# Two sets of edges, the second sorted on VectorE between the additions of the first set's chunks

## The chip, the cores and the metric

The kernel runs on one core of a Trainium2 chip. The metric is the device time of one execution, in microseconds (us). The core has four engines that compute: TensorE (PE in the profile), VectorE (DVE), ScalarE (ACT) and GpSimd (POOL); SyncE (SP) only issues DMAs. Each runs its own queue of instructions in order and waits on semaphores for the others.

## The reference

A graph attention layer with a residual and a layer norm: 6250 nodes of 128 features, 206250 edges in no order of use to the kernel.

```python
wn_out = n_out @ W_lin + b_lin
e_ij = leaky_relu2(jnp.concatenate([n_in, n_out], axis=-1) @ W_att + b_att)
a_ij = (e_ij @ w_alpha)[:, 0]
seg_max = jax.ops.segment_max(a_ij, recv, num_segments=N_NODES)
a_exp = jnp.exp(a_ij - seg_max[recv])
denom = jax.ops.segment_sum(a_exp, recv, num_segments=N_NODES)
alpha = a_exp / jnp.maximum(denom[recv], 1e-12)
n_i = jax.ops.segment_sum(alpha[:, None] * wn_out, recv, num_segments=N_NODES)
return jax.nn.elu(n_i)
...
x = _layernorm(x + _L0_gnn_ref(x, edge_attr_128, edge_index_t, L0_gnn_W_lin, L0_gnn_b_lin, L0_gnn_W_att, L0_gnn_b_att, L0_gnn_w_alpha), axis=-1)
```

## The kernel before

The receivers are 49 blocks of 128 nodes. The kernel sorts the edges by the receiver's block, so that each unit of 128 places in the sorted order belongs to one block, and then goes through the units in order, four at a time (a chunk of 512 places).

**Ahead of the loop.** The edges are packed as keys in a tile of 128 partitions by 2048 columns. VectorE sorts it by a bitonic network of min and max operations: phases 1 to 10 inside groups of columns, then 14 runs. An even run compares across all columns (11 stages, most of them in two halves, `within`); an odd run compares across partitions (run s of them has s stages), for which PE turns the tile by transposes and ScalarE copies it back (`piece_out`), half by half. `compare` issues one min and one max; `compare_groups` two of each over half as many elements. Within run 0 stands `make_padding`: ScalarE has counted the edges of each block in 49 passes (`count_pass`), PE has summed the counts, and VectorE works out how many pad places each block needs; the pads go through DRAM into the key tile. At the same time PE and ScalarE make a table in DRAM, for each node its part of the hidden vector and its `wn_out` (`project`, `copy_pqv`), and the receivers' part in SBUF, which is split into three bf16 parts by VectorE and ScalarE during the sort (`split_p`).

**The loop.** 415 chunks; each engine has its own `step(i, j)`, run for chunk k = 8 i + j by `chunks`: eight steps written out, a hardware loop of eight steps a body, and the last seven written out. The engines work on different chunks in the same step:
- GpSimd: `gather`, four indirect DMAs that fetch the table's rows of 512 senders into `rows`, a ring of eight chunks. It waits for `indexed` and for `high_sums_done` of the chunk eight before.
- PE: `high_sums(k)`, `hidden(k + 4)`, `turn_weights(k + 1)`, `mask(k + 3)`, `low_sums(k + 1)`, `spread_lanes(k + 6)`. `hidden` waits for the gathered rows.
- ScalarE: `weigh(k + 2)`, `slope(k + 4)`, `copy_weights(k + 1)`, `lessen(k + 2)` (two activations), `stage_index(k + 9)`.
- VectorE: `lowest(k + 2)`, the first addition `add_sums(k, 0)`, `new_peaks(k + 2)` (a scan), the second addition, `leaky_relu(k + 3)`, the third addition, `grow(k + 2)`, `make_onehot(k + 5)`, the fourth addition. An addition scales and adds one unit's sums (from PSUM) into `sums` of its block.

The last units hold only pads, whose senders all point to one block of 128 rows of the table. Behind the loop come the division, elu, the residual and the layer norm, block by block.

Lines of the profile: L412 is `gather`'s indirect DMA; L1020 lowest, L1028 the scan, L1036 `grow`, L1012 `leaky_relu`, L1006 `make_onehot`, L1049 an addition; L899 and L900 are min and max of `compare`, L907 and L908 of `compare_groups`; L644 turns a piece of the tile, L493, L494 and L487 copy it back; L431 counts, L614 and L615 are `project`; L825 begins `make_padding`; L991 to L996 unpack the sorted keys at the end of the sort.

## Time and profile before

| | us |
|---|---|
| median of 3 runs (2672.36 to 2678.7) | 2672.62 |
| the profiled execution's own time | 2676.63 |
| its span, first to last instruction | 2674.9 |
| PE busy | 2265.2 (85%) |
| VectorE busy | 1938.0 (72%) |
| ScalarE busy | 1338.6 (50%) |
| GpSimd busy | 1584.3 (59%) |

The busy times are of one profiled execution. Issuing and waiting are not counted as busy, and the ends of matmuls are modelled. The clock that TensorE was granted is 2.4 GHz in nearly the whole loop (1.0 in the profile) and 1.2 GHz (0.5) from about 250 to 530 us.

### The profile page before, as it was taken

The page shows a single profiled execution, that of the slowest core. Times are in us where ns is not written, and L with a number is a line of the kernel's source. Part 1 is how long each engine was busy: PE and PEld are TensorE (multiplying, and loading weights), DVE is VectorE, ACT ScalarE, POOL GpSimd, SP SyncE. Part 2 cuts the span into 40 slices and gives each one's busy share as a digit, 9 for nine tenths or more (in the row PEclk, how much of TensorE's full clock was granted, in tenths as well). Part 3 has the DMA queues.
Part 4 walks back from the last instruction along what each step waited for, and adds up shares of the span by engine and source line. Part 5 has one row for each costly group of instructions (what it writes and reads, how often), then busy time and mean ns, then how long its engine had stood idle before and what let it go on. Part 6 is the DMA issues. An engine that isn't in the chain of part 4 may idle for free.

```text
span 2674.9 us, 67073 instructions
## 1 busy us (share of the span) xinstructions
PE 2265.2 (85%) x13543; PEld 1535.4 (57%) x13752; DVE 1938.0 (72%) x4727; ACT 1338.6 (50%) x4146; POOL 1584.3 (59%) x1674
## 2 busy tenths in 40 slices
PE   3991211199999999999999999999999999999981
PEld 1330111166666666666666666666666666666661
DVE  7978999866666666666666666666666666666667
ACT  3772111055555555555555555555555555555545
POOL 0000000277777777777777777777777777777760
PEclk9998555599999999999999999999999999999996
DMA  4110000043333333333333333333333333333361
GB/s 103 39 41 19 0 0 0 22 108 105 105 106 104 105 105 104 106 105 105 106 104 105 105 104 106 105 105 106 105 105 105 104 105 106 104 106 105 105 93 50
DMA packets 96368, 235.57 MB, mean 88 GB/s; under 512 B 27935, under 2 KB 41205, under 8 KB 96135
## 3 DMA queue, kind: packets, MB, share of 16 engines
q0 software_dynamic: 79744, 218.60, 31.3%
q1 hardware_dynamic: 16594, 16.65, 2.2%
q8 instruction: 10, 0.16, 0.0%
q14 instruction: 20, 0.16, 0.0%
HBM read 225.32 MB, written 9.82 MB: 88 GB/s over the span
## 4 chain that ended last, share of the span: by engine, by line
PE 80%; DVE 11%; issue 4%; DMA 2%; POOL 2%; ACT 1%; DVEq 0%; SPq 0%; POOLq 0%; ACTq 0%
PE hidden_ps L675 24%; PE turned_ps L702 14%; PE masked_ps L686 14%; PE turned_ps L693 8%; PE hidden_ps L672 8%; DVE keys_i L900 4%; DVE keys_i L899 4%; PE turned_ps L660 3%; PE hidden_ps L615 3%; PE hidden_ps L614 2%; PE masked_ps L685 2%; POOL rows L412 2%; DMA rows<-qv_table,index 1%; DMA x_sb<-in_x 1%; PE masked_ps L608 1%
## 5 line engine op out<-in xcount | busy, mean ns | idle before, releaser
L412 POOL DMA_INDIRECT rows<-qv_table,index x1660 | 1576.1, 949 | 557.5 <-issue 476.5
L531 ACT ACTIVATE keys_i<-masked_ps,peaks 128x128 f32<-128x128 f32 x1660 | 474.5, 368 | 602.4 <-DVE peaks L1028 602.4
L675 PE MATMUL hidden_ps<-onehotT,p_part 128*128 128x128 bf16 x4980 | 740.4, 220 | 1.4
L1020 DVE TENSOR_REDUCE unit_low<-masked_ps 128x4 f32<-128x512 f32 x415 | 287.1, 692 | 594.8 <-PE masked_ps L686 594.8
L675 PEld LDWEIGHTS hidden_ps<-onehotT,p_part 128*128 x4980 | 472.2, 96 | 275.5 <-issue 205.1
L702 PEld LDWEIGHTS turned_ps<-rows,keys_i 128*128 128x128 f32 x3320 | 456.8, 190 | 299.5 <-issue 269.3
L1049 DVE SCALAR_TENSOR_TENSOR sums<-sums,shrink,turned_ps 128x129 f32 x1660 | 572.5, 345 | 66.3 <-issue 2.9
L702 PE MATMUL turned_ps<-rows,keys_i 128*128 128x129 f32 x3320 | 523.0, 280 | 15.1 <-issue 11.6
L672 PE MATMUL hidden_ps<-identf,rows 128*128 128x128 f32 x1660 | 470.4, 283 | 15.7 <-DMA rows<-qv_table,index 10.7
L686 PE MATMUL masked_ps<-leaky,w_cols 128*128 128x512 f32 x830 | 424.9, 593 | 10.9
L522 ACT ACTIVATE keys_i<-hidden_ps 128x512 f32<-128x512 f32 x415 | 247.9, 597 | 319.7 <-PE hidden_ps L675 319.5
L1006 DVE TENSOR_SCALAR onehotT<-turned_ps,part_f 128x512 bf16<-128x512 f32 x415 | 309.3, 745 | 13.8 <-PE turned_ps L660 7.5
L1012 DVE TENSOR_TENSOR leaky<-hidden_ps,keys_i 128x512 f32<-128x512 f32 x415 | 283.8, 684 | 0.0
L693 PE MATMUL turned_ps<-identf,keys_i 128*128 128x128 f32 x1660 | 261.0, 280 | 0.5
L672 PEld LDWEIGHTS hidden_ps<-identf,rows 128*128 128x128 f32 x1660 | 231.6, 140 | 44.2 <-issue 28.7
L550 ACT ACTIVATE keys_i<-turned_ps 128x512 f32<-128x512 f32 x415 | 247.9, 597 | 5.7 <-PE turned_ps L693 3.6
L644 PE MATMUL turned_ps<-identf,keys_i 128*128 128x128 f32 x208 | 50.0, 420 | 234.0 <-DVE keys_i L900 197.0
L693 PEld LDWEIGHTS turned_ps<-identf,keys_i 128*128 128x128 f32 x1660 | 174.6, 141 | 20.8 <-issue 2.3
L644 PEld LDWEIGHTS turned_ps<-identf,keys_i 128*128 128x128 f32 x208 | 39.9, 220 | 243.8 <-DVE keys_i L900 170.2
L686 PEld LDWEIGHTS masked_ps<-leaky,w_cols 128*128 128x128 f32 x830 | 158.2, 191 | 15.6
L660 PE MATMUL turned_ps<-lane_rows,identb 128*128 128x512 bf16 x414 | 157.5, 380 | 5.1 <-DVE onehotT L1006 5.1
L398 POOL MEMSET sums<- 128x6321 f32 x1 | 5.4, 5367 | 235.1 <-ACT p_part L507 235.1
(133 smaller groups left out, 1618.5 us busy)
## 6 DMA issues: line engine op xcount, KB each, us to landing
rows<-qv_table,index POOLq DMA_INDIRECT x1660
qv_table<-qv_out SPq DMA_DIRECT2D x49, 128.5 KB, 2.3
out<-x_sb SPq DMA_DIRECT2D x1, 1344.0 KB
recv_mem<-unit_blocks SPq DMA_DIRECT2D x1, 896.0 KB, 5.2
out<-x_sb SPq DMA_DIRECT2D x1, 896.0 KB
keys_i<-in_src SPq DMA_DIRECT2D x1, 768.0 KB
keys_i<-in_dst SPq DMA_DIRECT2D x1, 768.0 KB
recv_mem<-in_src SPq DMA_DIRECT2D x1, 604.5 KB
```

Source lines behind the costliest of these rows:

```text
L412: g.indirect_dma_start(out=rows[:, j % U, c, :], out_offset=None, in_=table, in_offset=bass.IndirectOffsetOnAxis(ap=index[:, j % U, c:c + ...
L522: a.activation(sloped[:, j % 2, :], hidden_ps[:, j % 2, :], ACT.Copy, scale=SLOPE).then_inc(sloped_ready, 1)
L531: last = a.activation(weightsT[:, j % 2, unit], masked_ps[:, j % 2, unit], ACT.Exp, bias=peaks[:, bass.ds(k * PER + i + 1, 1)])
L672: t.matmul(whole[:, unit], rows[:, j % U, c, 0:F], identf[:], is_transpose=True, start=True, stop=False, skip_group_check=True)
L675: mm = t.matmul(whole[:, unit], p_parts[s][:, bass.ds(of[c // SUB], F)], onehotT[:, j % 4, unit], start=False, stop=(s == 2), skip_group_c ...
L686: t.matmul(whole, w_cols[:], leaky[:, j % 2, :], start=False, stop=True).then_inc(masked_done, 1)
L693: mm = t.transpose(weights_ps[:, c * P:(c + 1) * P], weightsT[:, j % 2, c * P:(c + 1) * P], identf[:])
L702: mm = t.matmul(unit_sums_ps[:, i, :], weights[:, j % 2, c * P:(c + 1) * P], rows[:, j % U, c, F:R], start=(c == i * SUB), stop=(c == (i + ...
L1006: v.tensor_scalar(onehotT[:, j % 4, :], spread_ps, part_f[:], None, ALU.is_equal).then_inc(onehotT_ready, 1)
L1012: v.tensor_tensor(leaky[:, j % 2, :], hidden_ps[:, j % 2, :], sloped[:, j % 2, :], ALU.max).then_inc(leaky_ready, 1)
L1020: v.tensor_reduce(unit_low[:], masked_ps[:, j % 2, :].rearrange("p (i e) -> p i e", i=PER), AX_X, ALU.max, negate=True).then_inc(unit_low_ ...
L1049: v.scalar_tensor_tensor(out=at, in0=at, scalar=shrink[:, j % 4, i:i + 1], in1=unit_sums_ps[:, i, :], op0=ALU.mult, op1=ALU.add).then_inc( ...
```

## The change

The tile of 2048 columns is replaced by two sets. Set A is the first 121 x 1024 edges, set B the other 82346. Each has its own tile of 1024 columns, its own pads, counts, blocks of units and list of senders. Set A is sorted ahead of the loop and gives 254 chunks; set B is sorted in between and gives 173; together 427. `UNROLLED` is 256: PE, ScalarE and VectorE have the steps of the first 256 chunks written out, GpSimd the first eight as before.

Set B's sort is a generator, `second_sort`. Each `yield` ends a step: 4 of preparation, 45 of phases 1 to 9 (two `compare_groups`, four operations of 256 elements), 1, 11 of padding (seven of them with seven scalar_tensor_tensor operations of 56 elements), then 14 runs of 101 stages in all, with two empty steps between runs. 80 of the run stages are a `compare` of 1024 columns (two operations of 512 elements), 21 are `compare_groups`. Eleven steps stand in the first sort (`FILLING`); from chunk 1 on VectorE issues one a chunk, between the second and the third addition, up to chunk 181. For the turns between runs PE's transposes stand at the end of one step and behind `high_sums` in the next, and ScalarE copies at the end of a step and behind `slope` in the next (`aside_run`); they use the PSUM bank of `weights_ps`, so `turn_weights` waits for the copy.

At chunk 251 (`BOUNDARY`) PE and ScalarE bring the lowest value that set A found for each block into a form that set B's scan reads: eight transposes of peaks before and there, eight small products that sum to one, and products that spread it over units, each copied by ScalarE before the next. `new_peaks` scans eight elements a chunk for it instead of four, and `lessen` is one activation instead of two. Counting of set B: 24 passes in the first sort, 25 on ScalarE in chunks 1 to 25. The table is made two blocks at a time (`table_pair`), five pairs among the counts of set A, five behind them, 15 behind runs of the first sort; its bias is added as bf16 parts, and p is split into its three parts there by PE and ScalarE (`split_p` is gone). x - 1 moves from the front into the loop on ScalarE. The set A padding compares all block ends at once (`reached`, 56 x 49 elements) instead of in 49 operations.

The diff, cut to its core (`...` marks what is left out):

```diff
+    W = 1024
+    PIECE = W // 2
+    LOCAL = W.bit_length() - 1
+    PHASES = LOCAL + P.bit_length() - 1
+    RUNS = 2 * (PHASES - LOCAL)
...
+    EDGE_ROWS = [P - PROWS, 0]
+    E_A = EDGE_ROWS[0] * W
+    E_B = E - E_A
+    ROWS_B, REST_B = E_B // W, E_B % W
+    EDGE_ROWS[1] = ROWS_B + 1
+    UNITS_A = (E_A + PAD_PLACES) // UNIT
+    NA = UNITS_A // PER
+    NBC = -(-((E_B + PAD_PLACES) // UNIT) // PER)
+    UNITS_B = NBC * PER
+    NCH = NA + NBC
+    SLOTS = W // P
+    AHEAD = 4
+    UNROLLED = -(-NA // U) * U
+    LOOPED = (NCH - AHEAD - 1) // U
...
+    UP = 11
+    PREPARING = 4
+    PADDING = 11
+    GAP = 2
+    run_ends, step = [], PREPARING + LOCAL * (LOCAL - 1) // 2 + 1 + PADDING
+    for run in range(RUNS):
+        step += stages_of(run)
+        run_ends.append(step - 1)
+        step += GAP
+
+    def chunk_of(step):
+        return step - UP + 1
+
+    TOTALS_AT = 28
+    turn_low = {chunk_of(run_ends[run]) + 1: run for run in range(RUNS - 1)}
+    turn_high = {at + 1: run for at, run in turn_low.items()}
...
+    TABLE_BEFORE = [5, 6, 7, 8, 9]
+    TABLE_BEHIND = {1: [10, 11], 3: [12, 13], 5: [14, 15], 6: [16], 7: [17, 18], 8: [19], 9: [20, 21], 10: [22], 11: [23, 24]}
+    COUNTS_BEHIND = {1: 3, 3: 3, 5: 3, 7: 3, 9: 3, 11: 3, 12: 6}
+    COUNTED_UP = sum(COUNTS_BEHIND.values())
+    FILLING = {1: 2, 2: 2, 3: 1, 4: 1, 5: 1, 7: 1, 9: 1, 11: 1, 13: 1}
...
-        def chunks(eng, step):
-
-            def body(i, n):
-                for j in range(n):
+        def chunks(eng, step, unrolled):
+
+            for k in range(unrolled):
+                step(k // U, k % U)
+            with eng.Fori(unrolled // U, LOOPED) as i:
+                for j in range(U):
                     step(i, j)
-
-            body(0, U)
-            with eng.Fori(1, BODIES) as i:
-                body(i, U)
-            body(BODIES, NCH - BODIES * U)
...
-            chunks(pool, gather)
+            chunks(pool, gather, U)
...
-                    act.wait_ge(shrink_ready, k)
-                a.activation(eased[:], growth[:, j % 4, :], ACT.Relu).then_inc(eased_ready, 1)
                 if past(k, 4):
                     act.wait_ge(sums_ready, (k - 3) * PER)
-                act.wait_ge(eased_ready, k + 1)
-                a.activation(shrink[:, j % 4, :], eased[:], ACT.Exp, scale=-1.0).then_inc(shrink_ready, 1)
+                a.activation(shrink[:, j % 4, :], growth[:, j % 4, :], ACT.Exp, scale=-1.0).then_inc(shrink_ready, 1)
...
+            def aside_run(run, h):
+                act.wait_ge(aside_ps, aside_of_run(run, h))
+                piece_out(run, weights_ps, keys[1][:, 1 - ends_in[run], h * PIECE:(h + 1) * PIECE]).then_inc(aside_out, 1)
...
-                    weigh(k + 2, j + 2)
+                    weigh(i, j + 2)
                 if real(k + 4):
                     slope(k + 4, j + 4)
+                if isinstance(i, int) and k in turn_high:
+                    aside_run(turn_high[k], 1)
                 if real(k + 1):
                     copy_weights(k + 1, j + 1)
                 if real(k + 2):
                     lessen(k + 2, j + 2)
                 if real(k + U + 1):
...
+            def aside_run(run, h):
+                if h == 0:
+                    pe.wait_ge(run_done[1], run + 1)
+                pe.wait_ge(aside_out, aside_of_run(run, h) - 1)
+                for c in range(C):
+                    at = h * PIECE + c * P
+                    mm = t.transpose(weights_ps[:, c * P:(c + 1) * P], keys[1][:, ends_in[run], at:at + P], identf[:])
+                mm.then_inc(aside_ps, 1)
+                return aside_of_run(run, h)
...
+                    pe.wait_ge(blk_packed[1], 4)
+                if real(k + 4):
+                    of = blocks_of(mybir.EngineType.PE, i, j + 4, F)
                 high_sums(k, j)
+                if unrolled and k in turn_high:
+                    asides = aside_run(turn_high[k], 1)
                 if real(k + 4):
-                    hidden(k + 4, j + 4, i + 1 + (j + 4) // U, held[j])
+                    hidden(k + 4, j + 4, i + 1 + (j + 4) // U, of)
                 if real(k + 1):
                     turn_weights(k + 1, j + 1)
                 if real(k + 3):
                     mask(k + 3, j + 3)
...
+                    v.tensor_tensor(reached, pad_up[:].unsqueeze(2).to_broadcast([P, PC, NB]),
+                                    need_ends[:].unsqueeze(1).to_broadcast([P, PC, NB]), ALU.is_ge).then_inc(passing[0], 1)
+                    dve.wait_ge(passing[0], 1)
+                    v.tensor_reduce(pad_block[:, 0, :], reached, AX_X, ALU.add).then_inc(passing[0], 1)
...
+                done, now = 0, 0
+                sorting = slice(0, EDGE_ROWS[1])
+                for phase in range(1, LOCAL):
+                    for stage in reversed(range(phase)):
+                        if done:
+                            dve.wait_ge(compared[1], done)
+                        for r in (0, 1):
+                            compare_groups(keys[1][sorting, now, :], keys[1][sorting, 1 - now, :], 1 << stage,
+                                           1 << phase, r).then_inc(compared[1], 1)
+                        done, now = done + 2, 1 - now
...
+                for run in range(RUNS):
+                    if run:
+                        for gap in range(GAP):
+                            if run == 5 and gap == 0:
+                                pack_blocks(1)
+                            if run == 5 and gap == 1:
+                                find_fresh(1)
+                            yield
+                        now = starts_in[run]
+                        dve.wait_ge(aside_out, aside_of_run(run - 1, 1))
+                        sorting = slice(0, P)
+                    stages, phase = stages_of(run), phase_of(run)
+                    for n in range(stages):
+                        dve.wait_ge(compared[1], done)
+                        src, dst = keys[1][sorting, now, :], keys[1][sorting, 1 - now, :]
+                        if run % 2 == 0:
+                            last = compare(src, dst, W >> (n + 1))
+                        elif n >= phase - LOCAL:
+                            last = compare(src, dst, W >> (n - (phase - LOCAL) + 1))
+                        elif phase == PHASES:
+                            last = compare(src, dst, 1 << (phase - LOCAL - 1 - n))
+                        else:
+                            compare_groups(src, dst, 1 << (stages - 1 - n), 1 << stages, 0)
+                            last = compare_groups(src, dst, 1 << (stages - 1 - n), 1 << stages, 1)
+                        now = 1 - now
+                        if n < stages - 1:
+                            last.then_inc(compared[1], 1)
+                            done += 1
+                        else:
+                            last.then_inc(run_done[1], 1)
...
 
             def step(i, j):
                 k = i * U + j
+                unrolled = isinstance(i, int)
                 if real(k + 2):
-                    lowest(k + 2, j + 2)
-                if j % EACH == 0:
-                    for n, of in enumerate(blocks_of(mybir.EngineType.DVE, i, j)):
-                        held[j + n] = of
-                of = held[j]
+                    lowest(i, j + 2)
+                if unrolled and k == NA:
+                    dve.wait_ge(blk_packed[1], 4)
+                of = blocks_of(mybir.EngineType.DVE, i, j)
                 add_sums(k, j, 0, of)
                 if real(k + 2):
-                    new_peaks(k + 2, j + 2)
-                if PER > 2:
-                    add_sums(k, j, 1, of)
+                    new_peaks(i, j + 2)
+                add_sums(k, j, 1, of)
                 if real(k + 3):
                     leaky_relu(k + 3, j + 3)
-                add_sums(k, j, PER // 2, of)
+                if unrolled and chunk_of(steps) == k <= LANES_AT + 1:
+                    second_on(1)
+                add_sums(k, j, 2, of)
                 if real(k + 2):
-                    grow(k + 2, j + 2)
+                    grow(i, j + 2)
                 if real(k + 5):
                     make_onehot(k + 5, j + 5)
-                if PER > 2:
-                    add_sums(k, j, 3, of)
-
-            chunks(dve, step)
+                add_sums(k, j, 3, of)
+
+            chunks(dve, step, UNROLLED)
```

## Rows read from the trace of the kernel before

**Rows 1.** Busy time by engine in the loop (sum, count), granted clock, DMA share, GB/s.

```profile
560.00:2560.00 2000.00, 1971.90 (x12572) 1382.01 (x12770) 1375.01 (x3591) 1090.72 (x3595) 1513.44 (x1597) 1.00 0.39 105
```

**Rows 2.** Timeline of VectorE, lowest of four chunks (start, us, instruction, [idle before <-releaser]).

```profile
552.30 0.69 DVE L1020 TENSOR_REDUCE unit_low<-masked_ps 128x4 f32<-128x512 f32 x1 [0.64 <-PE masked_ps L686]
...
565.38 0.69 DVE L1020 TENSOR_REDUCE unit_low<-masked_ps 128x4 f32<-128x512 f32 x1 [1.00 <-PE masked_ps L686]
```

**Rows 3.** Waits from 700 to 2200 us: us in total, times, longest.

```profile
POOL rows L412 <- issue: 343.3, 1126, 0.3
```

**Rows 4.** Timeline of GpSimd in the loop, first and last of 1030 gathers.

```profile
1308.87 0.94 POOL L412 DMA_INDIRECT rows<-qv_table,index  x1 [0.30 <-PE turned_ps L702]
...
2598.36 0.95 POOL L412 DMA_INDIRECT rows<-qv_table,index  x1 [0.30 <-issue]
```

**Rows 5.** Timeline of VectorE, one step of the loop.

```profile
1201.79 0.69 DVE L1020 TENSOR_REDUCE unit_low<-masked_ps 128x4 f32<-128x512 f32 x1 [1.47 <-PE masked_ps L686]
...
1204.03 0.34 DVE L1049 SCALAR_TENSOR_TENSOR sums<-sums,shrink,turned_ps 128x129 f32 x1
...
1206.78 0.69 DVE L1020 TENSOR_REDUCE unit_low<-masked_ps 128x4 f32<-128x512 f32 x1 [1.42 <-PE masked_ps L686]
```

**Rows 6.** Timeline of VectorE ahead of the loop: first compare, and counts.

```profile
34.47 1.05 DVE L907 TENSOR_TENSOR keys_i<-keys_i 101x512 f32<-101x512 f32 x1
...
203.79 0.21 DVE L825 COPY sign_sums<-turned_ps 128x50 f32<-128x50 f32 x1 [22.90 <-PE turned_ps L634]
```

**Rows 7.** Timeline of VectorE in the sort: 256 elements, then 512.

```profile
274.62 0.42 DVE L908 TENSOR_TENSOR keys_i<-keys_i  x1
274.96 0.42 DVE L907 TENSOR_TENSOR keys_i<-keys_i  x1
...
487.06 0.69 DVE L899 TENSOR_TENSOR keys_i<-keys_i  x1
487.67 0.69 DVE L900 TENSOR_TENSOR keys_i<-keys_i  x1
488.50 0.69 DVE L899 TENSOR_TENSOR keys_i<-keys_i  x1
```

**Rows 8.** Groups by line up to 640 us (busy us, mean ns), and a DMA's landing.

```profile
L431 ACT ACTIVATE lane_rows<-lanes,thresholds 128x1612 bf16<-128x1612 bf16 x49 | 80.3, 1639 | 0.0
L614 PE MATMUL hidden_ps<-w,xT 128*128 128x384 f32 x98 | 73.2, 850 | 0.2 <-ACT xT L445 0.2
...
keys_i<-pads POOLq DMA_DIRECT2D x1, 32.0 KB, 2.5
```

**Rows 9.** Timeline of one turn between runs of the sort.

```profile
239.34 1.97 PE L644 MATMUL turned_ps<-identf,keys_i 128*128 128x128 f32 x8 [1.83 <-DVE keys_i L900]
...
242.77 0.61 DVE L907 TENSOR_TENSOR keys_i<-keys_i  x1 [1.36 <-ACT keys_i L494]
```

**Rows 10.** Last chunks: window as rows 1, and lowest of two chunks.

```profile
2580.00:2590.00 10.00, 7.53 (x46) 5.08 (x45) 5.33 (x14) 4.54 (x17) 7.56 (x9) 1.00 1.00 80
...
2587.99 0.69 DVE L1020 TENSOR_REDUCE unit_low<-masked_ps 128x4 f32<-128x512 f32 x1 [3.06 <-PE masked_ps L686]
...
2594.60 0.69 DVE L1020 TENSOR_REDUCE unit_low<-masked_ps 128x4 f32<-128x512 f32 x1 [3.04 <-PE masked_ps L686]
```

**Rows 11.** Timeline: L808 early in the front, then the handover to the gathers.

```profile
30.15 2.29 DVE L808 TENSOR_TENSOR keys_i<-keys_i 128x2048 int32<-128x2048 int32 x1
...
517.38 1.23 DVE L994 TENSOR_SCALAR lanes<-senders 128x2048 bf16<-128x2048 int32 x1
517.46 2.04 POOL L412 DMA_INDIRECT rows<-qv_table,index  x1 [51.75 <-ACT index L515]
518.64 2.29 DVE L996 TENSOR_TENSOR lanes<-lanes,keys_i 128x2048 bf16<-128x2048 bf16 x1
519.81 1.97 POOL L412 DMA_INDIRECT rows<-qv_table,index  x1 [0.31 <-issue]
```

1068 lines of the change are left out of this document (645 added, 423 removed).

## The prediction

> **What bounds the kernel now.** I read the windows first, then the waits, then the timeline engine by engine. The loop over chunks runs from about 520 to 2600 us of a 2674.9 us span. The chain of waits puts 80% of the span on PE, and the window of the loop shows PE busy for 1971.9 of 2000 us [rows 1]. That reading misleads: ends of matmuls are modelled, and just after the start, where gathered rows were in store, four chunks came 13.08 us apart over three steps, 4.36 us each [rows 2]. In the steady loop the bound is POOL. It issues four indirect DMAs (gathers) for a chunk; its only idle time is "issue", 0.30 us before 1126 of about 1200 of them [rows 3]; and from the gather at 1308.87 to the last, at 2598.36, 1029 gathers take 1289.5 us: 1.253 us each, 5.012 a chunk, with no slow one between [rows 4]. VectorE takes 4.99 us from one lowest to the next, of which it waits 1.42 us for PE [rows 5]: 3.57 us of work. PE has about 0.65 us and VectorE 1.4 us to spare in each chunk; POOL has none.
>
> Ahead of the loop VectorE is the bound: the sort starts at 34.47 and waits 22.9 us for the counts at 203.79 [rows 6]; the first gather starts at 517.46 [rows 11]. From the end of the last one (2599.3) to the end of the span it is 75.6 us.
>
> **The change, part by part.**
>
> *More chunks.* 254 + 173 = 427 instead of 415, at 5.012 us: 2140.1 against 2080.0, **+60 us**.
>
> *A shorter first sort.* A set of 1024 columns instead of 2048 halves each operation and drops a phase. On VectorE independent min and max operations of 512 elements start 0.61 us apart (487.06 to 487.67), of 256 elements 0.34 (274.62 to 274.96); one of 512 that waits for the one before starts 0.83 behind it (487.67 to 488.50) [rows 7]. Hence 0.20 for 128 elements (estimate, by the same slope), and a lone dependent pair of 256 takes 0.9. The sum in time:
> - Start: 14, an estimate between 10 (the small preparations alone) and 34.5 (nothing gained). Two DMAs of 0.5 MB go first, and nothing waits for `recv` any more.
> - Phases 1 to 9: 45 stages x 4 x 0.335 = 60.3, and 3 for phase ends: 78.
> - Counting on ScalarE: a pass of 1612 columns takes 1.64 us [rows 8]; scaled, 1.1 for 1024, 49 passes 54 us, five table pairs inside at about 3: totals at 83. VectorE reaches `padding` at 87, so the wait of 22.9 us is gone.
> - Padding 10 us (two operations over 56x49 elements are 6 of it), pads out and in again, two landings of up to 2.5 us [rows 8]: 102. What is late next is the table: five pairs between totals and the first turn, PE-bound at two products of 1.49 us (146 matmul halves, 0.85 us mean) [rows 8] and small ones, 4.7 us a pair: the first turn at 105.
> - Then 13 runs. A piece of eight transposes took 1.97 us, and 3.5 us passed from the last compare to the next engine's start (239.3 to 242.77) [rows 9]; with four transposes and half the copy 2.2. An even run to the end of its first half is 1.4 + 1.8 + 9.4 = 12.6 us; an odd run of s stages adds 2.2 + 2.06 s + 2.1. The eleven steps of the second sort that stand here cost little ahead of even runs, where VectorE would wait 2 us, and about 1 to 1.7 us each ahead of odd ones; packing and `fresh` cost 4. First halves then end at 121, 144, 168, 198, 227 and 257; the last run with its three whole stages at 277.
> - Unpacking and the first index copy: first gather at 282. It was 517.5: **-235 us**. Splitting p in three and x - 1 leave ScalarE's and VectorE's front; they were beside other work, save 14.5 us on VectorE, which are in these numbers.
>
> *PE's and ScalarE's extra work in the loop.* For each of 13 turns eight transposes (two times 0.6 us) and a wait: the copy of the second half stands on ScalarE behind `slope`, which waits for `hidden`, so `turn_weights` comes about 1.4 us later. That is 2.8 us per turn; turns are about 12 chunks apart, and PE wins back 0.65 a chunk. Cost **0**: POOL, which runs up to eight chunks (40 us) ahead, had its buffer free about 13 us early (the last gather of the chunk whose lowest starts at 1206.78 is the 91st before 1308.87, so it ended at 1195.8, 11.0 us earlier; that chunk's last sums come two steps later, 10.9 us more: 26.6 us after its first gather began) [rows 4, 5]. Passes of counting (1.3 us a chunk, 25 chunks) fit into ScalarE's idle 2.2 us.
>
> *The boundary.* The last six chunks gather pad rows only: DMA engines 100% busy at 80 GB/s, chunks 6.6 us apart (2587.99 to 2594.60) [rows 10]. After the change this comes twice, and at chunk 251 PE also stands still for some 8 us (eight products, three copies, in turn). 10 + 8 is 5 more than the 13 us of store: **+5**.
>
> *VectorE's stage in the chunk.* It is 2 x 0.61 or 4 x 0.34 us: 1.2 or 1.35, at most 1.6 in seven padding steps. 3.57 + 1.35 = 4.9 is under 5.01. Between the second and third addition it delays `add_sums` 2 and 3, `grow` and the one-hot rows: on VectorE's queue these three and the next lowest wait for it. VectorE has done all of them 1.42 us before PE ends `mask` [rows 5], and PE takes up the sums and the one-hot rows only behind `mask` and the low sums, so up to 1.4 us the placement costs **0**. Nothing of it is in SP's or POOL's queue.
>
> *What the stage does to POOL.* The trace has one place where gathers and VectorE operations on two SBUF operands meet: at the handover L996 (two operands in SBUF) runs from 518.64 to 520.93; the gather that starts at 519.81 takes 1.97 us instead of 0.95 and ends 0.85 behind L996. The one at 517.46 takes 2.04 and ends 0.89 behind L994 (517.38 to 518.61) [rows 11]. So a gather that starts in such an operation waits for its end. A compare has both operands in SBUF, and POOL has nothing to spare, so each such wait is paid in full. Bounds: nothing, if the case of 519.81 was something else; and the whole stage, 1.35 us a chunk, if no gather gets in between its operations. If it gets in between two operations, an operation of length s delays the gathers by s*s/(2 x 1.252) on average: 0.29 us for two of 0.6, 0.18 for four of 0.34. With 80 and 59 such steps: 23 + 11 = **34 us**. I take this: two separate instructions are nearer to two cases like L996 than to one. If the stage counts as one, gathers that start in it are thrown behind it, VectorE follows POOL at a fixed distance, and the delay D feeds back. The stage starts 2.24 us behind lowest, 13.2 behind the last gather's end; the 10th, 11th or 12th gather after that one would start at 11.6, 12.8 or 14.1, plus 2 D. With 1.3 us of stage 3 D = 14.5 - 11.6 (or 12.8, 14.1): D is 0.97, 0.57 or 0.13. Followed chunk by chunk the first comes out most often: 147 us.
>
> The Trainium skill (SBUF — State Buffer, Who interferes with whom) says that tensor_tensor with two SBUF inputs contends with GpSimd's reads only, and infers that it does not stall descriptor generation. By that the cost is nothing; the row of 519.81 speaks against it. The same section says that whichever starts first holds the pair for its whole instruction.
>
> **Sum.** 282 + 2 (slow first gathers) + 2140 + 75.6 + 5 = 2505 of span, + 34 = 2539. The profiled run took 2676.63, 1.7 over its span, and 4.0 over the median, so the median should be near **2537 us**, 5.1% below 2672.62.
>
> **Rivals.**
> - *A: gathers are not held up at all* (the first rule above): 2503. For it: 415 chunks without one slow gather, though VectorE was busy 69% of the time, with one SBUF operand or tiny ones. Against: the two rows. Chance 0.12.
> - *B: the whole stage shuts POOL out*: 2505 + 147, 2650. Operations start 0.61 apart while each lasts 0.69, so the next holds on before the last lets go. Against: nothing in the trace. Chance 0.29; with smaller delays it ends anywhere from 2540 to 2650.
> - *C, slower: each holds the other out.* If a gather in flight also stops VectorE for its 0.95 us, operations and gathers alternate: 4 x (0.34 + 0.95) or 2 x (0.6 + 0.95) in the stage, chunks of 8.7 and 6.7 us, 59 x 3.6 + 80 x 1.65 = 344 us more: 2847. It decides from 170 us, 1.2 us a chunk over the 139 steps. Against: L996 began in the middle of the gather of 517.46 and took 2.29 us, as L808 with the same sizes took with POOL idle [rows 11]. Chance 0.08; the skill's rule of the whole instruction would make it so.
> - *D: VectorE's or PE's 256 unrolled chunks run slower than the loop* (loading instructions) by more than the 0.65 us PE has. Chunks 4 to 6, unrolled, ran at 4.4 [rows 2]. It needs 0.65 + 0.55 us a chunk over 256 to undo the gain. Chance of slower than before 0.05, of a smaller loss 0.05.
>
> **How the numbers follow.** Forecast 0.41 (2515 to 2560, by 12 us on the front and 10 on the stage), A 0.12, B 0.29, C 0.08, D 0.10. The range leaves out C, half of D and the edges of A: 2490 to 2665. 0.3% is 8 us, about what a measurement tells from no change: faster 0.81, same 0.04 (from B's upper end and D), slower 0.15.
>
> **What would show it.** First gather at 282 plus or minus 12; no wait for the counts before `padding`. In chunks 1 to 180 gathers longer than 0.95 us whenever they start inside a compare, ending 0.85 behind it: behind the first of the pair for the forecast, behind the last for B, none for A; compares that start late behind a gather for C. From chunk 190 gathers 1.252 us apart, 20.05 us for four chunks. VectorE's idle time before lowest near zero with POOL waiting for nothing. Gathers waiting for `high_sums` only at the boundary; if they wait for it elsewhere, the store of 13 us is wrong and PE's turns are paid.

## The result and the profile after

The changed kernel takes 2514.53 us (2512.93 to 2515.42, four runs) against 2673.31 of the kernel before in the same comparison: ratio 0.9401, 95% interval 0.9385 to 0.9418, so 6.0% faster. The forecast was 2537. The profiled execution took 2515.42, span 2513.6.

From the page of the changed kernel: busy time by engine, then the span in 40 slices.

```profile
PE 2201.0 (88%) x14002; PEld 1568.5 (62%) x14217; DVE 1942.1 (77%) x5224; ACT 1293.6 (51%) x3890; POOL 1659.3 (66%) x1734
...
DVE  9999699987888887888866666676667676766757
...
POOL 2000477777777777777777777777777777777750
```

VectorE is as busy as before in total, but its sorting no longer stands alone ahead of the loop: POOL is at work from the fifth slice on, where it was idle to 517 us before [rows 11].

Timeline of GpSimd in the changed kernel, L517 its gathers: the first one, one beside a stage, one of many with nothing beside, and the last.

```profile
274.31 1.04 POOL L517 DMA_INDIRECT rows<-qv_table,index  x1 [169.87 <-ACT index L603]
...
594.15 1.41 POOL L517 DMA_INDIRECT rows<-qv_table,index  x1 [0.30 <-issue]
595.86 0.95 POOL L517 DMA_INDIRECT rows<-qv_table,index  x1 [0.30 <-issue]
...
1308.23 0.95 POOL L517 DMA_INDIRECT rows<-qv_table,index  x1 [0.30 <-issue]
...
2433.29 0.95 POOL L517 DMA_INDIRECT rows<-qv_table,index  x1 [0.30 <-issue]
```

From 1308.23 to the last, 900 gathers take 1125.1 us: 1.250 each, 5.00 a chunk, as [rows 4]. The 768 gathers of chunks 0 to 191 take 985.2 us, 25 more than 768 times 1.250; added up one by one, what the long ones have over 0.947 us is 24.8. So all that the second sort costs the loop stands in the lengths of gathers, none of it in waits between them.

Where the time went, by differences of the two traces: first gather 517.5 to 274.3, **-243.2**; twelve more chunks **+60**; long gathers **+24.8**; and from the last gather's end to the end 79.4 against 75.6, **+3.8**. The rest, some 7 us less, is a rate of 5.00 for 5.012 and the slow first gathers that are gone.

### The profile page after: what moved, and what is told of

Read it like the earlier page. It is cut to its first block, busy times and chain, and to the rows that moved or that the text cites. A ratio compares the mean times of both kernels' runs of the same rounds, so it can differ in the third digit from the quotient of the medians.

```text
span 2513.6 us, 64106 instructions
## 1 busy us (share of the span) xinstructions
PE 2201.0 (88%) x14002; PEld 1568.5 (62%) x14217; DVE 1942.1 (77%) x5224; ACT 1293.6 (51%) x3890; POOL 1659.3 (66%) x1734
## 4 chain that ended last, share of the span: by engine, by line
PE 65%; DVE 9%; POOL 9%; issue 8%; DMA 5%; ACT 4%; DVEq 0%; POOLq 0%; ACTq 0%
PE hidden_ps L816 20%; PE masked_ps L827 12%; PE turned_ps L846 12%; POOL rows L517 9%; PE turned_ps L838 7%; PE hidden_ps L813 7%; DMA rows<-qv_table,index 5%; PE turned_ps L801 3%; ACT rows L530 2%; DVE keys_a L1110 2%; DVE keys_a L1111 2%; PE masked_ps L826 1%; DVE keys_a L1118 1%; DVE keys_a L1119 1%; PE turned_ps L862 1%
## 5 line engine op out<-in xcount | busy, mean ns | idle before, releaser
L517 POOL DMA_INDIRECT rows<-qv_table,index x1708 | 1639.9, 960 | 689.9 <-issue 484.7
L620 ACT ACTIVATE keys_a<-masked_ps,peaks 128x128 f32<-128x128 f32 x1708 | 487.0, 368 | 692.6 <-DVE peaks L1361 690.6
L846 PEld LDWEIGHTS turned_ps<-rows,keys_a 128*128 128x128 f32 x3416 | 491.4, 191 | 283.3 <-issue 122.2
L1383 DVE SCALAR_TENSOR_TENSOR sums<-sums,shrink,turned_ps 128x129 f32 x1708 | 587.9, 344 | 85.4 <-issue 24.8
L846 PE MATMUL turned_ps<-rows,keys_a 128*128 128x129 f32 x3416 | 536.1, 280 | 12.0 <-issue 6.4
L610 ACT ACTIVATE sloped<-hidden_ps 128x512 f32<-128x512 f32 x427 | 255.3, 598 | 324.0 <-PE hidden_ps L816 318.9
L1348 DVE TENSOR_REDUCE lows_a<-masked_ps 128x4 f32<-128x512 f32 x254 | 174.9, 689 | 201.2 <-PE masked_ps L827 200.4
L1348 DVE TENSOR_REDUCE lows_b<-masked_ps 128x512 f32 (+1 forms) x173 | 119.7, 692 | 232.5 <-PE masked_ps L827 232.5
L1332 DVE TENSOR_TENSOR leaky<-hidden_ps,sloped 128x512 f32<-128x512 f32 x427 | 292.2, 684 | 1.6
L838 PE MATMUL turned_ps<-identf,keys_a 128*128 128x128 f32 x1708 | 269.6, 281 | 18.0 <-ACT keys_b L579 9.3
L635 ACT ACTIVATE keys_a<-turned_ps 128x512 f32<-128x512 f32 x427 | 255.0, 597 | 17.3 <-PE turned_ps L838 15.9
L838 PEld LDWEIGHTS turned_ps<-identf,keys_a 128*128 128x128 f32 x1708 | 180.5, 141 | 38.6 <-issue 21.1
L827 PEld LDWEIGHTS masked_ps<-leaky,w_cols 128*128 128x128 f32 x854 | 163.9, 192 | 16.4
```

Of the source, the lines that this page charges most:

```text
L517: g.indirect_dma_start(out=rows[:, j % U, c, :], out_offset=None, in_=table, in_offset=bass.IndirectOffsetOnAxis(ap=index[:, j % U, c:c + ...
L610: a.activation(sloped[:, j % 2, :], hidden_ps[:, j % 2, :], ACT.Copy, scale=SLOPE).then_inc(sloped_ready, 1)
L620: last = a.activation(weightsT[:, j % 2, unit], masked_ps[:, j % 2, unit], ACT.Exp, bias=peaks[:, bass.ds(peaks_of(i, j) + 2 + 2 * n, 1)])
L827: t.matmul(whole, w_cols[:], leaky[:, j % 2, :], start=False, stop=True).then_inc(masked_done, 1)
L838: mm = t.transpose(weights_ps[:, c * P:(c + 1) * P], weightsT[:, j % 2, c * P:(c + 1) * P], identf[:])
L846: mm = t.matmul(unit_sums_ps[:, c, :], weights[:, j % 2, c * P:(c + 1) * P], rows[:, j % U, c, F:R], start=True, stop=True)
```

## The experiments

Where not said otherwise a kernel is the changed one with one edit. The kernel before took 2675.15 us beside e1 to e4, 2672.40 beside e9 and e10, 2671.62 beside e11 and e12; times without a ratio are read against these.

### e1: the stage behind the fourth addition

```diff
-                if unrolled and chunk_of(steps) == k <= LANES_AT + 1:
-                    second_on(1)
                 add_sums(k, j, 2, of)
                 ...
                 add_sums(k, j, 3, of)
+                if unrolled and chunk_of(steps) == k <= LANES_AT + 1:
+                    second_on(1)
```

> The stage of the second sort is moved behind the fourth addition of its chunk; everything else is as in the changed kernel (2514.5 us). Theory 1 (GpSimd is the bound; what the stage costs are the gathers that start inside a compare, wherever it stands): VectorE reaches the same work in the same chunk, its next lowest comes at most 1.4 us later, which PE has to spare, so the placement itself costs nothing; only the point of the gathers' rhythm at which the compares fall moves, so the 25 us of long gathers may become anything from 15 to 40: 2505 to 2530. Rival (VectorE or PE is the bound in the chunks with a stage, and the placement hides the stage in a wait of VectorE): lowest is 1.3 us late in 139 chunks and this is paid, at least in part: over 2560, up to 2695.

Measured: 2546.49 (2541.01 to 2551.35), ratio 0.9520 (0.9507 to 0.9533): 32 us slower than the changed kernel and between the two ranges. By the number neither theory has it; by where the time is lost it is theory 1, with more lost than its 40 us: first gather 273.8, last part unchanged, and the long gathers of chunks 0 to 191 add up to 56.3 us instead of 24.8. All 32 us are there. But they are not longer by chance of the rhythm alone. Timeline of this kernel, GpSimd and the compares of one stage:

```profile
319.32 0.42 DVE L1118 TENSOR_TENSOR keys_b<-keys_b 81x256 f32<-81x256 f32 x1
319.66 0.42 DVE L1119 TENSOR_TENSOR keys_b<-keys_b 81x256 f32<-81x256 f32 x1
319.67 1.89 POOL L517 DMA_INDIRECT rows<-qv_table,index  x1 [0.30 <-ACT index L603]
319.99 0.42 DVE L1118 TENSOR_TENSOR keys_b<-keys_b 81x256 f32<-81x256 f32 x1
320.33 0.42 DVE L1119 TENSOR_TENSOR keys_b<-keys_b 81x256 f32<-81x256 f32 x1
320.66 0.68 DVE L1348 TENSOR_REDUCE lows_a<-masked_ps 128x4 f32<-128x512 f32 x1
```

The gather that starts with the second operation ends at 321.56, 0.81 behind the **last** of the stage, not behind the one it started in. Of the 131 gathers that waited in this kernel 36 waited for later operations of the stage, 30 us of the 56; in the changed kernel 1 of 111. In these counts, here and below, a gather that starts less than 0.1 us ahead of an operation counts with that operation; counted strictly by the operation in which it starts it is 43 here, 14 in e10, 38 in e11 and still 1 in the changed kernel. That is the mechanism of the prediction's rival B, in a quarter of the cases, and the place in the chunk decides how often.

### e2: shorter operations

The 80 `compare` stages of set B, 512 elements twice, become 256 four times:

```diff
-                            last = compare(src, dst, W >> (n + 1))
+                            last = compare_quarters(src, dst, W >> (n + 1))
...
+                for h in (0, 1):
+                    ...
+                    v.tensor_tensor(outs[:, ms, 0, ds], a, b, ALU.min)
+                    last = v.tensor_tensor(outs[:, ms, 1, ds], a, b, ALU.max)
```

> The 80 compare stages of set B are issued as four operations of 256 elements instead of two of 512; set A's sort is as it was. Theory 1 (a gather that starts inside a compare waits for the end of that one operation, and POOL pays it in full): the wait goes with the operation's length; the 16.7 us of long gathers in these 80 steps become about 8.6, by what the 59 four-operation steps show now (6.4 us), or 14 by the square of the length alone: 2506 to 2513. Rival 2 (a gather waits for the end of the whole stage): the stage gets longer by 0.12 us a step, so 80 x 0.12 = 10 us at most more, never less: 2515 to 2525. Rival 3 (VectorE's load is what costs): also more, 2515 to 2525.

Measured: 2504.03 (2501.91 to 2509.35), ratio 0.9367 (0.9354 to 0.9380), 10.5 us faster than the changed kernel though VectorE has more to do. Long gathers add up to 11.9 instead of 24.8. Rivals 2 and 3 expected a longer time and fall. It is theory 1, but with 2 us more than its range, and the traces show where more comes from than the shorter wait. A gather that starts within 0.03 us behind a compare's start is not always held; where it isn't, the compare takes some 0.05 us longer instead. Timeline of the changed kernel, the first compare of a stage with such a gather, and the second:

```profile
323.37 0.47 DVE L1118 TENSOR_TENSOR keys_b<-keys_b 81x256 f32<-81x256 f32 x1
323.38 0.95 POOL L517 DMA_INDIRECT rows<-qv_table,index  x1 [0.30 <-issue]
323.76 0.41 DVE L1119 TENSOR_TENSOR keys_b<-keys_b 81x256 f32<-81x256 f32 x1
```

There are 12 such gathers in the changed kernel, 52 in e2 and 1 in e1. That is chance of the rhythm, and how much of the 10.5 us it gave is not separated from what the shorter operations gave.

### e3: one operand instead of two

```diff
+                for t in (0, 1):
+                    last = v.tensor_reduce(outs[:, :, t, :], ins[:, :, t, :].unsqueeze(3), AX_X, ALU.max)
...
-                            last = compare(src, dst, W >> (n + 1))
+                            last = stay(src, dst, W >> (n + 1))
```

> Each min and max of set B's sort is replaced by a maximum over one element (tensor_reduce) with one operand in SBUF and as many elements out, so that the keys stay where they are; the comparing of set B is what is left out, its pads, counts, transposes and all other work remain. Theory 1 (the two SBUF operands of a compare keep a starting gather out): VectorE is as busy as before, no gather in chunks 1 to 180 is longer than 0.95, and the 25 us go: 2490. Rival 3 (VectorE's load or the memory traffic costs the 25 us): 2510 to 2520. Rival 4 (any VectorE operation on SBUF of this size does it, one operand or two): long gathers as before, 2510 to 2520.

Measured: 2480.89 (2479.49 to 2481.49). Timeline: two such operations, back to back, and a gather that starts in the second.

```profile
602.97 1.27 DVE L1139 TENSOR_REDUCE keys_b<-keys_b 81x512 f32<-81x512 f32 x2
603.86 0.95 POOL L517 DMA_INDIRECT rows<-qv_table,index  x1 [0.30 <-issue]
605.11 0.94 POOL L517 DMA_INDIRECT rows<-qv_table,index  x1 [0.30 <-issue]
```

The stage is as long, and the gather is not held. Long gathers add up to 2.1 us, 22.7 less. The expected 2490 missed 12 us that have another cause: set B is left unsorted, its last chunks no longer gather pads alone (DMA engines 40% busy near the end instead of 85%), and the stretch behind the last gather takes 67.2 us instead of 79.4. 22.7 + 12.2 are 34.9, 33.6 were measured. Rivals 3 and 4 fall: it is not VectorE's load, and a tensor_reduce of this size does not do it. That it is the second operand in SBUF and not the kind of operation is shown by L1332 of the changed kernel, a tensor_tensor with one operand in PSUM: 111 gathers start in it, and 109 of them take 0.95 us.

The other two, and about half of the 2.1 us left over here, show what the expectation did not have: a tensor_scalar with a single tensor operand, over 1024 columns of SBUF, lengthens gathers too, even one that is already under way. In the changed kernel the gather of 500.86 starts in L1332, L1169 starts 0.36 us behind it, and the gather ends 0.12 us behind L1169:

```profile
500.86 1.22 POOL L517 DMA_INDIRECT rows<-qv_table,index  x1 [0.30 <-issue]
...
501.22 0.74 DVE L1169 TENSOR_SCALAR keys_b<-keys_b,sign_of 81x1024 f32<-81x1024 f32 x1
```

Such operations are rare in the loop. So the second operand in SBUF explains what the compares do, but an operation with one is not safe in general.

### e4: ten filling steps moved into the loop

```diff
-    UP = 11
+    UP = 1
...
-    FILLING = {1: 2, 2: 2, 3: 1, 4: 1, 5: 1, 7: 1, 9: 1, 11: 1, 13: 1}
+    FILLING = {1: 1}
```

> Ten of the eleven steps of the second sort that stand in the first sort are moved into the loop, one a chunk as the others (the first stays, ScalarE's counting of set B needs it). Prediction's prices: a filling step costs 1.0 to 1.7 us ahead of an odd run (8 steps, seven of them moved) and little ahead of an even one, so the front gets 7 to 12 us shorter; in the loop each step costs 0.11 us by the 59 four-operation steps now, 1 to 2 us: 2504 to 2509. Rival 5 (PE's table pairs and turns bound the front, the filling stands in VectorE's waits for them): the front is unchanged, and the loop loses 1 to 2 us: 2515 to 2517. Rival 3 (VectorE's load in the loop costs 1.3 us a step): front -10, loop +13: 2517.

Measured: 2509.58 (2507.81 to 2510.08), ratio 0.9380 (0.9367 to 0.9393), 5 us faster than the changed kernel. First gather at 264.5 instead of 274.3: a filling step costs the front 0.98 us; in the loop the long gathers come to 25.5 instead of 24.8. The time is 0.6 us above the expected range. The front's price is as expected (7 to 12), the loop's too; the last 2 us are in the part behind chunk 191 (1175.6 instead of 1173.8).

### e5 to e8: rows that landed late

> hidden adds two of the three bf16 parts of the receivers' product: the third part's four products of 128 columns in each chunk are what is left out on PE (48 of them took 0.15 us each, so about 0.6 us a chunk, 256 us over 427 chunks). Theory 1 (POOL is the bound in every chunk, the chain of waits shows PE only because it follows the gathers): the gathers keep their 5.00 us a chunk, 2510 to 2516, at most 4 us gained at the boundary and in the last chunks. Rival 6 (PE, 94 to 97% busy in the windows, is a bound of its own): chunks come down to about 4.6 us, 2350 to 2450.

> POOL issues three gathers a chunk instead of four; the fourth unit's products read the third unit's rows, so a quarter of the senders' rows is what is left out. POOL then needs 3.76 us a chunk. Theory 1: what is next late is PE, by the prediction's 4.36 us a chunk where rows were in store, and VectorE with a stage in the chunk, 3.57 + 1.35 = 4.9: chunks of 4.9 in the first 181 and of 4.4 behind it, 274 + 181 x 4.9 + 246 x 4.4 + 80 = 2323; 2290 to 2350. Rival 6 (PE or VectorE is as late as POOL already): over 2450, no gain to speak of. No gather length matters any more in either case.

> The stage stands behind lowest and ahead of the first addition. In the changed kernel (2514.5) a gather that starts in a compare waits for that one operation, behind the fourth addition (2546.5) 39 of the gathers waited for later operations of the stage too. Theory 1a (the gathers are only let in between two compares where VectorE came to the stage with a free engine in between, not out of a row of four operations back to back): here the stage follows lowest, for which VectorE waits on PE, so it is like the changed kernel: 2505 to 2525, few gathers behind more than one operation. Theory 1b (it is chance of the rhythm, whatever the place): anywhere from 2505 to 2550, with gathers thrown further. Rival 7 (new_peaks comes 1.3 us later, and weigh, turn_weights and the sums of PE wait for it): PE has 0.65 us to spare and 1.3 are lost: 2514 + 139 x 0.65 = 2600.

> The stage stands between make_onehot and the fourth addition, one addition (0.26 us) ahead of the place behind it that cost 2546.5. Theory 1b (the rhythm decides which gathers are thrown behind the whole stage): the stage is followed by an addition with its wait long over, as in the changed kernel, but starts where the slow place does: somewhere from 2510 to 2550. Theory 1c (what follows the stage decides: lowest behind it, an addition behind it here and in the changed kernel): few gathers thrown behind more than one operation, 2505 to 2525. Theory 1d (it is a place behind the long one-hot operation and an addition, so late in the chunk, that is bad): 2540 to 2550.

These four ran on a chip where gathered rows landed late for every kernel: the kernel before took 3769.27 us there, and their times (3627.83, 2739.33, 3629.27, 3583.25) tell nothing of these theories. In e5 a chunk's lowest comes some 34 to 40 us behind the end of its last gather (11 elsewhere), and POOL waits for the ring of eight to come free. Waits of e5 between 2000 and 2400 us (us in total, times, longest):

```profile
POOL rows L517 <- PE turned_ps L846: 137.3, 26, 6.3
```

Why the rows landed late there is open. One thing can be counted all the same, which operation a held gather waited for. e7: none of 56 behind a later operation of its stage. e8: 4 of 119.

### e9: both gains together

The edits of e2 and of e4 in one kernel.

> Both gains together: set B's 80 compares of two operations issued as four operations of 256 elements (2504.0 alone), and ten of the eleven filling steps moved into the loop (2509.6 alone), against 2514.5 for the changed kernel. Theory 1: the gains lie in different stretches (gathers in the loop; VectorE in the first sort) and add up: 2514.5 - 10.5 - 4.9 = 2499, 2496 to 2503, with the first gather at 264 to 265 and some 13 us of long gathers. Rival 3 (VectorE's load in the loop matters): ten more steps of 1.35 us and 0.12 us more in each of the 80 make it late, 2505 or more.

Measured: 2495.17 (2493.90 to 2499.79), ratio 0.9336 (0.9323 to 0.9349): 19 us faster than the changed kernel, 177 faster than the kernel before, and the best of this study. First gather at 265.0, long gathers 16 us where 13 were expected (33 gathers of the kind shown in e2, 52 there). The time is 0.8 us below the range: the gains add up at least to their sum of 15, and the rivals' 2505 or more falls.

### e10: the stage ahead of the fourth addition

```diff
                 if real(k + 5):
                     make_onehot(k + 5, j + 5)
+                if unrolled and chunk_of(steps) == k <= LANES_AT + 1:
+                    second_on(1)
                 add_sums(k, j, 3, of)
```

> The same kernel as e8_ahead_of_fourth, on a chip where gathers are again 5.0 us a chunk apart if there is one: there every kernel took 7.2 to 8 us a chunk, since gathered rows landed late, and gave no time to compare; but of 119 gathers that started in a compare only 4 waited for more than that one operation, against 36 of 131 with the stage behind the fourth addition. If what follows the stage decides (an addition here and in the changed kernel, lowest behind the fourth): 2505 to 2525, at most 5 gathers thrown further. If the rhythm or the late place decides: 2535 to 2550, 20 or more thrown further.

Measured: 2522.13 (2519.27 to 2523.29), ratio 0.9436 (0.9423 to 0.9449): 8 us slower than the changed kernel, 24 faster than e1, from which it differs by the place of one addition. 4 of its 120 held gathers waited for a later operation (e1: 36 of 131); by the strict count 14 against 43. Long gathers 32.4 us. As expected by the theory that what follows the stage decides, and against the theory of a late place.

### e11: a memset between the stage and lowest

```diff
                     second_on(1)
+                    v.memset(between[:, k % 8:k % 8 + 1], 0.0)
```

> The stage stands behind the fourth addition as in e1_behind_fourth (2546.5, 36 gathers thrown behind a later operation of the stage), with one memset of 128x1 (some 0.06 us) behind it, ahead of the next lowest. Theory 1c in its narrow form (lowest, standing directly behind the stage, is what keeps gathers from getting in between two compares): few thrown gathers, 2510 to 2530. Theory 1e (what matters is something else of that place: that the stage comes right behind the fourth addition, or that the stage of one chunk is the last thing ahead of a wait for PE): as before, 30 or more thrown, 2540 to 2555.

The edit is e1's with the memset behind the stage. Measured: 2574.86 (2564.98 to 2577.40), ratio 0.9638 (0.9625 to 0.9651), above both ranges. 33 of 129 held gathers waited for a later operation of the stage, as in e1: lowest right behind the stage is **not** what does it. The long gathers add up to 52.0. The other 24 us lie where no stage runs at all, and are a finding of their own (last section).

### e12: three gathers a chunk

```diff
-                for c in range(C):
+                for c in range(C - 1):
                     g.indirect_dma_start(
```

> As e6_three_gathers: three gathers a chunk instead of four, a quarter of the senders' rows is what is left out. Theory 1: POOL needs 3.76 us a chunk and is no longer last; PE comes next by the prediction's 4.36 us a chunk, and VectorE with a stage in the chunk by 4.9: 2290 to 2350, with gathers waiting for high_sums. Rival 6 (PE is as late as POOL already): over 2450.

The fourth unit's products read the third unit's rows, so a quarter of the senders' rows is left out. Measured: 2343.72 (2342.58 to 2345.83), in the expected range. With a quarter of POOL's work gone the kernel gains 171 us, so POOL was the bound, and what is next late shows. Timeline of lowest: four chunks apart without a stage in the written-out steps; one chunk apart in the hardware loop.

```profile
1282.94 0.69 DVE L1348 TENSOR_REDUCE lows_a<-masked_ps 128x4 f32<-128x512 f32 x1 [0.37 <-PE masked_ps L827]
...
1299.77 0.69 DVE L1348 TENSOR_REDUCE lows_a<-masked_ps 128x4 f32<-128x512 f32 x1 [0.55 <-PE masked_ps L827]
...
2002.94 0.69 DVE L1348 TENSOR_REDUCE lows_b<-masked_ps 128x512 f32 x1 [0.82 <-PE masked_ps L827]
2007.39 0.69 DVE L1348 TENSOR_REDUCE lows_b<-masked_ps 128x512 f32 x1 [0.76 <-PE masked_ps L827]
```

Over 48 chunks from 192 on the written-out steps take 4.26 us each, behind chunk 256 the looped ones 4.64; in both lowest waits for PE. The first 192 chunks, with the stages in them, take 4.86 on average (932.7 us), and up to 5.2 over 16 chunks in the runs. So beside a stage the next engine is close behind POOL, and only the store of rows covers the chunks that are over POOL's 5.0.

## Why the prediction was right, point by point

**Bound by POOL: right.** Gathers 5.00 us apart in every stretch without a stage, while the windows of that stretch show PE at 98% (columns as [rows 1]):

```profile
1300.00:2400.00 1100.00, 1077.61 (x6957) 767.15 (x7066) 758.97 (x1980) 549.06 (x1771) 831.93 (x881) 1.00 0.39 106
```

e12 settles that this 98% is no bound. The prediction's 4.36 us for PE, taken at the start of the loop [rows 2], is 4.26 in written-out steps and 4.64 in looped ones: where the store of rows must be won back in looped steps, PE gains 0.36 us a chunk, not 0.65.

**The front: right in kind, 8 us too long.** First compare forecast at 14, measured at 14.59; end of the phases 78, measured 78.5. Waits of VectorE up to the first gather:

```profile
DVE keys_a L1110 <- ACT keys_a L574: 8.3, 5, 1.9
DVE sign_sums L1026 <- PE turned_ps L769: 3.2, 1, 3.2
```

The counts were late after all (3.2 us where none was forecast): a counting pass was put at 1.1 us, its rows start 1.27 apart:

```profile
86.29 1.15 ACT L530 ACTIVATE rows<-rows,thresholds 128x1024 bf16<-128x1024 bf16 x1
...
87.57 1.15 ACT L530 ACTIVATE rows<-rows,thresholds 128x1024 bf16<-128x1024 bf16 x1
```

49 times 0.17 are the 8 us from 83 to about 91 for the totals. Only 3.2 of them are a wait, as VectorE reached the padding at 87.7 in place of 87. The first turn came at 108.5, not 105, and what was late there was the table, as the prediction had it: VectorE's last compare ahead of it ended at 106.3, and PE went from the table's last small products (L751, from 108.34) into the turn without a pause. The second turn waited for VectorE.

```profile
105.89 0.42 DVE L1111 TENSOR_TENSOR keys_a<-keys_a 121x256 f32<-121x256 f32 x1
...
108.46 1.04 PE L781 MATMUL turned_ps<-identf,keys_a 128*128 128x128 f32 x8
...
111.13 0.66 PE L781 MATMUL turned_ps<-identf,keys_a 128*128 128x128 f32 x4 [1.63 <-DVE keys_a L1119]
```

The table was the other mis-sized term, and its error makes up for half of that of the counts: five pairs took 18 us behind the totals, 3.5 each for 4.7. In the changed kernel a product of L741, the counterpart of [rows 8]'s L614, takes 0.85 to 0.97 us where the granted clock is 0.50 (1.2 GHz, from 85 to 92 us) and 0.49 to 0.56 where it is 1.00 (2.4 GHz, from 97 to 107). From 92 to 111 us the clock was 0.88 on average, and the means from 85 to 115 us are 0.63 and 0.53 us (windows, columns as [rows 1], then groups: busy us, mean ns). In the kernel before L614 took 0.85 in the whole front, though the windows print a clock of 1.00 there; why is open. The prediction's count of 146 products is 98 in its row; the mean of 0.85 is the row's.

```profile
85.00:92.00 7.00, 1.87 (x5) 1.08 (x5) 3.68 (x14) 5.72 (x10) 0.00 (x0) 0.50 0.03 12
92.00:111.00 19.00, 14.01 (x65) 8.03 (x63) 17.05 (x36) 8.89 (x24) 2.42 (x4) 0.88 0.31 96
...
L741 PE MATMUL hidden_ps<-w,rows 128*128 128x384 f32 x12 | 6.5, 629 | 1.0 <-ACT rows L538 1.0
...
L741 PE MATMUL turned_ps<-w,rows 128*128 128x384 f32 x12 | 5.3, 527 | 0.1
```

From the first turn to the first gather it was 166 us, forecast 177. First halves ended at 126.7, 148.2, 170.8, 199.5, 225.8 and 254.0 (forecast 121 to 257): the first 2 us more behind the first turn than forecast, each further pair of runs 1.3 to 2.7 us shorter than the sum made of it, and from the last to the first gather 20 us in place of 25. Turns were overpriced: VectorE waits 9.9 us for six of them in all, the five above and one of 1.6; a filling step costs the front 0.98 us (e4), the lower end of what the prediction gave for those ahead of odd runs.

**PE's and ScalarE's extra work: right, 0.** POOL waits 22.5 us for `high_sums` in all 427 chunks, no wait over 0.3:

```profile
POOL rows L517 <- PE turned_ps L846: 22.5, 74, 0.3
```

Each of these stands in the 0.30 us that POOL spends between any two gathers.

**The boundary: +5 forecast, nothing measured.** POOL keeps its 75.6 us busy in each 100 us there:

```profile
1500.00:1600.00 100.00, 94.89 (x622) 70.40 (x632) 64.07 (x171) 48.68 (x157) 75.63 (x81) 0.98 0.40 107
1600.00:1700.00 100.00, 98.62 (x665) 71.32 (x674) 73.01 (x190) 52.47 (x171) 75.62 (x81) 1.00 0.40 106
```

The distance from a chunk's last gather to its lowest grows from 11.2 us (chunk 248) to 16.4 (chunk 256), 5 us where 18 were added up, inside the store of 13. Pads of one set and the products of the other do not follow each other with their full prices; which of the two was overpriced the runs don't separate.

**The placement: 0, right for where it was put, wrong in what it was argued from.** The argument was VectorE's and PE's time to spare. e1 has that too and loses 32 us, through POOL. The changed kernel's place is worth these 32 us, and e10's between the two, 8 and 24. That behind the fourth addition a gather is often let in only behind the last compare is shown; what decides it is not. It is not lowest as the next operation (e11), and not the late place alone (e10).

**The stage on POOL: right in mechanism, 34 forecast, 24.8 measured.** The gather of 594.15 above started in a compare of 594.06 to 594.74 and ended at 595.56, 0.82 behind it. So it was let in when the first operation ended, and did most of its work beside the stage's second one:

```profile
594.06 0.68 DVE L1110 TENSOR_TENSOR keys_b<-keys_b 81x512 f32<-81x512 f32 x1
...
594.66 0.68 DVE L1111 TENSOR_TENSOR keys_b<-keys_b 81x512 f32<-81x512 f32 x1
```

110 of 111 held gathers end 0.81 to 0.84 us behind the operation that they start in. Not every gather that starts in a compare is held: of 144 that do, 21 start in its last 0.18 us and lose under 0.03 us, and 12 start within 0.03 us behind its start (see e2). Per two-operation step this costs 0.21 us (16.7 us in 80), forecast 0.29; per four-operation step 0.10 (6.1 in 59), forecast 0.18. The mis-sized term is s in s*s/(2 x 1.252): the prediction put in the spacing of the operations, 0.61 and 0.335. But a gather that ends 0.82 behind an operation of 0.68 us has lost, against its own 0.947, 0.68 + 0.82 - 0.95 = 0.55 less the time from the operation's start to its own: here 0.55 - 0.09 = 0.46, as measured. For an operation of 0.42 us it is 0.29. The long gathers by their starts give 0.56 and 0.28 in place of 0.61 and 0.335, and with these the sum is 80 x 0.25 + 59 x 0.125 = 27, near the 25 measured. The prediction had the 0.85 and the 0.95 in its own rows [rows 11] and did not take their difference. One of its two rows was also not what it was taken for: L994, behind which the gather of 517.46 waited, is a tensor_scalar with one operand. Only the row of 519.81 is a case like a compare; the other belongs to the tensor_scalars of e3.

The Trainium skill (SBUF — State Buffer, Who interferes with whom) infers that tensor_tensor does not stall descriptor generation, since it takes only the read interface. The rows disagree: 111 gathers that start in one wait for its end. They agree with its other sentences there: an operation with two inputs in SBUF contends with a GpSimd instruction that reads SBUF, and tensor_reduce never does (e3). A compare does not stop a gather under way: none of the 118 gathers that start outside the compares and see one begin before their end takes more than 0.95 us. The tensor_scalar of e3 did.

**The rivals.** A (gathers not held, 2503) and C (each stops the other, 2847) are out: compares beside a gather keep 0.60 us from start to start, at most 0.65, and what a gather takes from a compare is 0.05 us where both start together (e2). B (the whole stage, 2650) is out in this place and true for a quarter of the cases in e1; its price was too high as well, since 139 stages at its own largest delay of 0.97 us are 135 us, not 147. D (unrolled code slower) is out: gathers stay 5.00 us a chunk apart in the written-out chunks 192 to 255, and in e12 these took PE 4.26 us, not more than the looped ones.

**The sum.** 2539 of span forecast, 2513.6 measured. Front -7.7, slow first gathers -1.9, rate -4.7, boundary -5, stage -9.2, behind the last gather +3.8: -24.7 of the 25.4. The +3.8 was not looked into. Nearly all errors have one sign, so the sum was not right by luck; only the counts and the table, +8 and -4 within the front, cancel in part.

## What to carry to other kernels

Where an engine that only issues transfers sets the rate, price a change by what it does to that engine's single instruction: which operands of the neighbour are in SBUF, and how long each of its operations is, not how busy the neighbour becomes. Cut the operations that hold it off into shorter ones even where that makes their own engine busier, and try the same stage in two or three places of the step, since places that are equal by every idle time can differ by 1%. Take away part of the bound's work once, to learn how far the next one is.

## What the runs showed of the hardware that was not expected

**A loop's way back cost VectorE nothing, 3 us or 5 us, in kernels that differ in how many instructions stand ahead of the loop.** VectorE's queue ends its written-out steps at chunk 255 and goes on in a hardware loop of eight chunks. Waits of lowest between 1700 and 2300 us, changed kernel:

```profile
DVE lows_b L1348 <- PE masked_ps L827: 156.2, 120, 1.6
```

The same of e9:

```profile
DVE lows_b L1360 <- PE masked_ps L827: 99.2, 90, 1.5
DVE lows_b L1360 <- issue: 44.7, 15, 3.4
```

And of e11, from 1700 to 2400 us:

```profile
DVE lows_b L1349 <- PE masked_ps L828: 107.0, 117, 1.7
DVE lows_b L1349 <- issue: 90.2, 17, 5.9
```

Once in eight chunks lowest waits for nothing that the profile shows, 3.0 us in e2 and e9, 5.3 in e11, nothing in the changed kernel, e1, e3, e4, e10 and e12. The loop's text is the same in all; what differs is the number of VectorE's instructions ahead of it (160 more in e2 and e9, 181 in e11, one for each stage, as many as before in the others). That it is how the loop's instructions are fetched is likely and was not tested. In e2 and e9 PE's time to spare covers it. In e11 it doesn't: chunks from about 310 on come 5.2 us apart, PE's granted clock falls from 1.00 to between 0.93 and 0.97, and that is the 24 us. A small edit far ahead of a loop can so cost more than what it edits, and an experiment that adds an instruction must be read stretch by stretch.

**PE's work of a chunk took 4.26 us written out and 4.64 in the hardware loop** (e12), with the same operations on the same shapes (seven lines of PE, their mean times within 0.01 us of each other). The looped chunks are also those of set B; the runs don't separate the two.

**Which of a gather and a compare waits is decided at the start, and hangs on hundredths of a microsecond.** Where both start together the gather can lose nothing and the compare 0.05 us (e2). e2 has 52 such gathers and 12 us of long ones, e9, the same with ten steps more in the loop, 33 and 16 us. What sets this rhythm is open.
